# A bound on the row gathers of two attention stages, with padding entries that point past the table

## The chip, the cores and the metric

One core of one Trainium2 chip. The metric is the device time of one execution in microseconds (us); the time of a kernel is the median of its runs.

## What is computed

Two layers over a graph of 6,250 nodes with 256 features and 106,250 edges, sorted by destination. Each layer is a graph attention and a mixture of experts, each added to x after a layer norm. The two attentions are what the change touches; cut to that:

```python
def _L0_gnn_ref(x, edge_index, W, att_src, att_dst, bias):       # 4 heads of 64
    h = (x @ W).reshape(N, HEADS, HEAD_DIM)
    e = leaky_relu(a_src[src] + a_dst[dst], 0.2)
    e = exp(e - segment_max(e, dst)[dst])
    alpha = e / segment_sum(e, dst)[dst]
    return segment_sum(alpha[:, :, None] * h[src], dst).reshape(N, 256) + bias

def _L1_gnn_ref(x, edge_attr, W1, W2, att_l, att_r, bias, src, dst):   # 1 head of 256
    score = leaky_relu(er[dst] + el)          # el: from x[src] and edge_attr
    alpha = softmax of score over the edges of one dst
    return segment_sum((x @ W2.T)[src] * alpha[:, None], dst) + bias

x = x + _L0_gnn_ref(_layernorm(x), ...)
x = x + _L0_ffn_ref(_layernorm(x), ...)       # 6 experts, the 2 best
x = x + _L1_gnn_ref(_layernorm(x), ...)
x = x + _L1_ffn_ref(_layernorm(x), ...)       # 8 experts, all
```

## The kernel before

The kernel runs in stages with a barrier after each: `rows(0)`, `attention(0)`, then routing, sorting and the picked experts, `rows(1)`, `attention(1)` and `dense_experts`. All of it is raw code on five engines, each with its own loop, held together by semaphores.

`rows(l)` writes a table `rows_d[l]` to device memory: one row for each node, 260 float32 in stage 0 (4 heads of 64 features, each with its source score) and 257 in stage 1, and one row more, number N = 6250, of zeros (`pad_row`, line 309). `rows(0)` also makes the edge list `edge_pack`: for each edge its source and its destination, and after the 106,250 edges another 256 entries of padding (`pad_pack`, lines 310 and 311) with source N and destination -1.

`attention(l)` takes the destinations in 50 tiles of 125. The edges of one tile are cut into units of 256 (`UE`), and a table holds where each unit starts and which tile it is for. The table has 464 units; those that no tile needs start at entry 106,250, so all their entries are padding. A slot of the loop is 8 units (`U`), and there are 58 slots (`SU`). The work of a slot is spread over five turns of the loop (`LAG`), in buffers for three slots (`RING`):

- SP loads the slot's entries into `pack` and its destinations into `drow`.
- POOL gathers the rows (line 687): 16 indirect DMAs for a slot, two for each unit, each of 128 rows by the 128 source indices of one column of `pack`, into `G`. Before the two gathers of a unit it waits (line 683) until the matmuls that read the same buffer three slots ago are done (`summed`).
- One turn later TensorE transposes the source scores that came with the rows (lines 734 and 735); in stage 0 it waits there for all rows of the slot, in stage 1 VectorE does so, adding the edge's own term (line 967).
- VectorE and ScalarE make a running maximum and the weight of each edge; an entry whose destination is in no tile has zeros in the incidence matrix (`MB`, line 959), so that it adds nothing.
- Two and three turns later TensorE multiplies incidence and weighted rows (line 720), and VectorE merges the sums into `acc` (line 926).

Two other places gather rows by an indirect DMA without any bound: line 1788 (128 rows of 256 float32, the picked experts' inputs) and line 318 (125 rows of 256 float32, in `rows(1)`).

```python
        for u in range(U):
            if late(i, RING):
                after(pool, p + "summed", i * U - U * RING + (u + 1))
            held(pool, p + "pool_seen")
            for q in range(u * C, (u + 1) * C):
                nc.gpsimd.indirect_dma_start(G[:, r, q, :], None, rows_d[l], ...)
```

Of the kernel before, what the change touches and what calls it, by code (L numbers as in the profile page):

```python
# [26 lines left out]
N = 6250  # L27
# [40 lines left out]
def build(nc, a, out):  # L68
    ctx = ExitStack()
    with ctx:  # L70
        def sb(name, shape, dt=F32, scope=ctx):
            return scope.enter_context(nc.sbuf_tensor(name, shape, dt))
# [4 lines left out]
        def S(name):  # L77

            if name not in sems:
                sems[name] = nc.alloc_semaphore(name=f"{name}_{stage[0]}")  # L80
            return sems[name]
# [8 lines left out]
        def after(eng, name, count):  # L90

            if not isinstance(count, int) or count > 0:
                eng.wait_ge(S(name), count)

        def held(eng, name):

            eng.sem_inc(S(name), 1)
# [49 lines left out]
        def late(i, k):  # L147

            return not isinstance(i, int) or i >= k
# [5 lines left out]
        def rows(l, acc, pos_i, share, sc):  # L155
# [6 lines left out]
            p = f"n{l}_"  # L162
# [9 lines left out]
            if l == 0:  # L172
# [6 lines left out]
                pad_pack = sb("pad_pack", [P, C, 2], I32, sc)  # L179
# [45 lines left out]
            with nc.Block() as block:  # L225
# [62 lines left out]
                @block.gpsimd  # L288
                def _(pool):
                    if l == 0:  # L290
                        nc.gpsimd.memset(ident[:, :], 0.0).then_inc(S("ident_zero"), 1)
                        nc.gpsimd.iota(int_n[:, :], pattern=[[1, P]], base=0, channel_multiplier=0)
                        nc.gpsimd.iota(int_nid[:, :], pattern=[[TN, NT]], base=0, channel_multiplier=1)
                        nc.gpsimd.iota(int_base[:, :], pattern=[[TN, NT]], base=0, channel_multiplier=0)
                        nc.gpsimd.iota(int_tile[:, :], pattern=[[1, NT]], base=0, channel_multiplier=0)
                        nc.gpsimd.iota(int_u[:, :], pattern=[[1, KU]], base=0, channel_multiplier=KU).then_inc(S("iotas"), 1)
                        pool.wait_ge(S("ident_zero"), 1)
                        nc.gpsimd.affine_select(out=ident[:, :], in_=ident[:, :], compare_op=ALU.not_equal, fill=1.0,
                                                base=0, pattern=[[-1, P]], channel_multiplier=1)
                        nc.gpsimd.memset(eps_ln[:, :], LN_EPS)  # L300
                        nc.gpsimd.memset(eps_bn[:, :], BN_EPS)
                        nc.gpsimd.memset(ones[:, :], 1.0)
                        nc.gpsimd.memset(zeros[:, :], 0.0)
                        nc.gpsimd.memset(cnt[:, :], 0.0).then_inc(S("fills"), 1)
                        nc.gpsimd.memset(pad_hl[:, 0, :], -1.0)
                        nc.gpsimd.memset(pad_hl[:, 1, :], 0.0)
                        nc.gpsimd.memset(ones_bf[:, :], 1.0)
                        nc.gpsimd.memset(pad_q[:, :], 0.0)
                        nc.gpsimd.memset(pad_row[:, :], 0.0)
                        nc.gpsimd.memset(pad_pack[:, :, 0:1], N)  # L310
                        nc.gpsimd.memset(pad_pack[:, :, 1:2].bitcast(F32), -1.0).then_inc(S("pads_set"), 1)
                    else:
                        for i in range(NG):
                            if i >= 4:
                                pool.wait_ge(S(p + "added"), i - 3)
                            for u in range(GT):
                                for k in range(2):
                                    nc.gpsimd.indirect_dma_start(yg[:, i % 4, u, k, :], None, y_d,
                                                                 bass.IndirectOffsetOnAxis(ap=pos_i[:, i * GT + u, k:k + 1], axis=0)).then_inc(S(p + f"yg_in{i % 4}"), 16)
# [226 lines left out]
        def attention(l, acc, sc):  # L546
# [5 lines left out]
            p = f"g{l}_"  # L552
# [6 lines left out]
            pack = sb(p + "pack", [P, RING, Q, 2], I32, sc)  # L559
# [55 lines left out]
            def run(eng, slot):  # L615

                for i in range(SU + LAG):
                    slot(i, i % RING, i // RING)

            def has(i, lag):  # L620

                return not isinstance(i, int) or lag <= i < SU + lag

            def filled(t, r, k, n):

                return (t + 1 - (k - r + RING - 1) // RING) * n
# [9 lines left out]
            with nc.Block() as block:  # L636
# [37 lines left out]
                @block.gpsimd  # L674
                def _(pool):
                    def slot(i, r, t):
                        if not has(i, 0):
                            return
                        pool.wait_ge(S(p + f"pack_in{r}"), filled(t, r, 0, 16 * U))
                        if isinstance(i, int) and i == RING - 1:  # L680
                            pool.wait_ge(S(p + "tab"), 6)
# [3 lines that stand above are left out]
                            held(pool, p + "pool_seen")  # L685
                            for q in range(u * C, (u + 1) * C):
                                nc.gpsimd.indirect_dma_start(G[:, r, q, :], None, rows_d[l],  # L687
                                                             bass.IndirectOffsetOnAxis(ap=pack[:, r, q, 0:1], axis=0)).then_inc(S(p + f"rows_in{r}"), 16)
                    run(pool, slot)

                @block.tensor
# [1256 lines left out]
```

## Time and profile before

| | us |
|---|---|
| median of 3 runs | 4523.83 (4523.54 to 4540.11) |
| span of the profiled execution | 4519.6 |
| attention stage 0, first to last gather | 174.8 to 1364.7 |
| attention stage 1, first to last gather | 2160.4 to 3348.9 |
| last matmul of the attention sums, stage 0 and 1 | 1416.2 and 3389.5 |

| engine | busy us | share of the span |
|---|---|---|
| TensorE (PE) | 3345.5 | 74% |
| VectorE (DVE) | 2669.4 | 59% |
| ScalarE (ACT) | 1569.3 | 35% |
| GpSimd (POOL) | 2042.6 | 45% |

The trace is of one execution, and its times count from the start of its span; the span is 4.2 us shorter than the median of the runs. A gather's entry on POOL is the time in which the instruction is worked on there, not the time until its rows have landed. "Idle before" is the time in which the engine had nothing to do before an instruction, with what ended it; "issue" there means that nothing the profile shows was waited for.

### The profile page before, as it was taken

To read this page: it belongs to the slowest core of one execution; us is meant where nothing else is said; L and a number is where in the kernel's file an instruction comes from. 1 tells how busy PE (TensorE), PEld (TensorE's weight loads), DVE (VectorE), ACT (ScalarE), POOL (GpSimd) and SP (SyncE) were. 2 spreads that over 40 slices of the span, in tenths; PEclk is the share of its full clock that TensorE was granted. 3 is DMA by queue.
4 is the path that set the end of the run, shared out by engine and by line. 5 is a ranking of instruction groups with operands and counts; after the bars stand their busy time and mean duration, and the time that the engine had idled before them with its cause. 6 is when DMAs were issued, how large, how long until landed. Compare 5 with 4: busy or idle time off the path is not lost. (4 is left out here: it accounts for less than half of the span.)

```text
span 4519.6 us, 72577 instructions
## 1 busy us (share of the span) xinstructions
PE 3345.5 (74%) x16240; PEld 2523.8 (56%) x16240; DVE 2669.4 (59%) x8449; ACT 1569.3 (35%) x4383; POOL 2042.6 (45%) x2095
## 2 busy tenths in 40 slices
PE   4366666666666789966366666666668999999999
PEld 3244444444444577744244444444447888888888
DVE  7489999999987866546356565656555322222221
ACT  2233333333332123332233333333323433343333
POOL 0377777777770033346677777777740000000000
PEclk9667777777776579977677777777778999999999
DMA  3344444444454135534444444444451000000000
GB/s 98 92 105 106 106 107 106 107 107 106 107 98 86 37 122 171 163 102 116 96 107 107 105 106 106 105 106 106 106 66 60 8 5 7 7 5 7 5 7 7
DMA packets 382598, 369.83 MB, mean 82 GB/s; under 512 B 249324, under 2 KB 309388, under 8 KB 382242
## 3 DMA queue, kind: packets, MB, share of 16 engines
q0 software_dynamic: 107072, 272.84, 24.4%
q1 hardware_dynamic: 272774, 92.39, 8.5%
q8 instruction: 102, 1.67, 0.2%
q14 instruction: 254, 2.08, 0.1%
q10 hardware_dynamic: 2396, 0.84, 0.1%
HBM read 324.13 MB, written 41.59 MB: 81 GB/s over the span
## 5 line engine op out<-in xcount | busy, mean ns | idle before, releaser
L687 POOL DMA_INDIRECT g_G<-rows,g_pack x1856 | 1807.9, 974 | 771.7 <-issue 487.0
L720 PE MATMUL bank<-g_G,g_MB 128*125 128x260 f32 x1856 | 663.3, 504 | 230.4 <-DVE acc L926 229.2
L926 DVE SCALAR_TENSOR_TENSOR acc<-acc,g_c,bank 125x65 f32 (+1 forms) x2320 | 618.5, 316 | 146.3 <-PE bank L720 71.1
L720 PE MATMUL bank<-g_G,g_M 128*125 128x257 f32 x1856 | 633.5, 489 | 20.7 <-DVE acc L926 20.5
L1367 DVE SCALAR_TENSOR_TENSOR X<-bank,e_cw,X 125x256 f32 (+1 forms) x400 | 175.2, 479 | 795.8 <-PE bank L1193 795.8
L720 PEld LDWEIGHTS bank<-g_G,g_MB 128*125 128x125 f32 x1856 | 422.8, 246 | 373.2 <-DVE acc L926 265.9
L1263 ACT ACTIVATE e_h<-bank,e_bi_c,e_sc_c 128x250 f32<-128x250 f32 x800 | 403.6, 555 | 560.6 <-PE bank L1184 422.3
L791 ACT ACTIVATE g_mt_d<-bank,unode 125x256 bf16<-125x256 f32 x928 | 381.9, 461 | 444.7 <-PE bank L705 444.5
L720 PEld LDWEIGHTS bank<-g_G,g_M 128*125 128x125 f32 x1856 | 418.1, 241 | 147.4 <-DVE acc L926 26.2
L1193 PE MATMUL bank<-e_w,e_h 128*125 128x256 f32 x1600 | 379.0, 380 | 3.1 <-ACT e_h L1263 3.1
L1184 PE MATMUL bank<-e_h,e_w 128*128 128x250 f32 x1600 | 377.8, 378 | 1.2 <-ACT e_h L1263 1.2
L1175 PE MATMUL bank<-e_xnT,e_w 128*128 128x250 f32 x1600 | 372.9, 375 | 0.0
L803 ACT ACTIVATE g_MT<-g_mt_d,ones 125x512 bf16<-125x512 bf16 x464 | 335.1, 722 | 11.4
L1193 PEld LDWEIGHTS bank<-e_w,e_h 128*125 128x125 f32 x1600 | 299.8, 187 | 47.5 <-ACT e_h L1263 3.9
L1175 PEld LDWEIGHTS bank<-e_xnT,e_w 128*128 128x128 f32 x1600 | 304.3, 190 | 36.5 <-issue 0.7
L1184 PEld LDWEIGHTS bank<-e_h,e_w 128*128 128x128 f32 x1600 | 297.7, 191 | 42.5 <-issue 8.0
L825 ACT COPY g_LT<-bank 64x128 f32<-64x128 f32 (+1 forms) x116 | 29.7, 256 | 833.2 <-PE bank L735 827.2
L959 DVE TENSOR_TENSOR g_MB<-iota_b,g_dloc 128x500 f32<-128x500 bf16 (+1 forms) x464 | 302.5, 674 | 0.1
L942 DVE TENSOR_TENSOR g_G<-g_G,bank 128x1024 f32<-128x1024 f32 x232 | 280.9, 1211 | 0.5 <-ACT bank L831 0.5
L734 PE MATMUL bank<-ident,g_b 128*16 128x128 f32 x58 | 21.5, 371 | 315.5 <-DVE g_dloc L972 301.0
L1788 POOL DMA_INDIRECT x_xg<-expert_in,ids x108 | 107.0, 990 | 288.6 <-PE bank L1804 190.4
L769 PE MATMUL bank<-g_rhs,g_MT 125*128 125x24 bf16 (+1 forms) x1856 | 66.3, 174 | 226.8 <-DVE g_rhs L1063 119.1
(299 smaller groups left out, 4151.2 us busy)
## 6 DMA issues: line engine op xcount, KB each, us to landing
g_G<-rows,g_pack POOLq DMA_INDIRECT x1856
acc<-in_edge_attr SPq DMA_DIRECT2D x50, 531.2 KB
g_pack<-edge_pack SPq DMA_DIRECT2D x928, 2.0 KB
g_drow<-edge_dst SPq DMA_DIRECT2D x928, 1.0 KB
expert_out<-x_y SPq DMA_DIRECT2D x54, 256.0 KB
g_qe<-edge_q SPq DMA_DIRECT2D x464, 1.0 KB
rows<-acc SPq DMA_DIRECT2D x25, 253.9 KB
rows<-n_T SPq DMA_DIRECT2D x25, 251.0 KB
```

The costliest lines, as they stand in the source:

```text
L687: nc.gpsimd.indirect_dma_start(G[:, r, q, :], None, rows_d[l], bass.IndirectOffsetOnAxis(ap=pack[:, r, q, 0:1], axis=0)).then_inc(S(p + f" ...
L720: mm_ = nc.tensor.matmul(sum_bank(r, k, u)[0:TN, 0:HW], left, G[:, rk, q, :], start=(c == 0), stop=(c == C - 1))
L791: ins = nc.scalar.activation(mt_d[:, v_ % 2, k * C:(k + 1) * C, :], bank[2 + v_ % 2][0:TN, k * UE:(k + 1) * UE].rearrange("p (e c) -> p c ...
L803: nc.scalar.activation(MT[:, turn(r, 1, v_), :, :], mt_d[:, v_ % 2, :, :], ACT.Relu, bias=ones[0:TN, 0:1], scale=-1.0).then_inc(S(p + "MT" ...
L926: ins = nc.vector.scalar_tensor_tensor(at, at, c1[:, rk, u, h:h + 1], sum_bank(r, k, u)[0:TN, h * W:(h + 1) * W], ALU.mult, ALU.add)
L942: ins = nc.vector.tensor_tensor(g[:, :, 0:DH], g[:, :, 0:DH], w, ALU.mult)
L959: nc.vector.tensor_tensor(MB[:, r, at, :], iota_b[:, 0:TN].unsqueeze(1).broadcast_to([P, CP, TN]), dloc[:, r, at, 0:1].broadcast_to([P, CP ...
L1175: mm = nc.tensor.matmul(bank[m][:, 0:GN], w1[:, e, k, m * P:(m + 1) * P], xnT[:, r, k, :], start=(k == 0), stop=(k == 1))
L1184: mm = nc.tensor.matmul(bank[2 + m][:, 0:GN], w2[:, e, k, m * P:(m + 1) * P], h1[:, k, :], start=(k == 0), stop=(k == 1))
L1193: mm = nc.tensor.matmul(bank[4 + u][0:TN, 0:D], h2[:, e % 2, k, u * TN:(u + 1) * TN], w3[:, e, k, :], start=(k == 0), stop=(k == 1))
L1263: ins = nc.scalar.activation((h1 if q == 0 else h2[:, e % 2, :, :])[:, m, :], bank[2 * q + m][:, 0:GN], ACT.Relu, bias=bi_c[:, q, m, e:e + ...
L1367: ins = nc.vector.scalar_tensor_tensor(xt, bank[4 + u][0:TN, 0:D], cw[:, r, u, e:e + 1], xt, ALU.mult, ALU.add)
```

## The change

The padding's source index becomes N + 1, and each gather of both attention stages gets a bound of N with the order to pass over an index beyond it instead of reporting an error. The row of an index that is passed over is not fetched, and its place in `G` keeps what it held. In the built program each of the 1,856 gathers has one instruction more ahead of it on POOL's queue: a register is set to 6250, and the gather names that register as its bound. No other instruction is added, removed or moved on any engine.

```diff
-                        nc.gpsimd.memset(pad_pack[:, :, 0:1], N)
+                        nc.gpsimd.memset(pad_pack[:, :, 0:1], N + 1)
...
                                 nc.gpsimd.indirect_dma_start(G[:, r, q, :], None, rows_d[l],
-                                                             bass.IndirectOffsetOnAxis(ap=pack[:, r, q, 0:1], axis=0)).then_inc(S(p + f"rows_in{r}"), 16)
+                                                             bass.IndirectOffsetOnAxis(ap=pack[:, r, q, 0:1], axis=0),
+                                                             bounds_check=N, oob_is_err=False).then_inc(S(p + f"rows_in{r}"), 16)
```

## Rows read from the trace of the kernel before

**Rows 1.** Windows: 400 us in the middle of stage 0 and stage 1, all engines.

```profile
core 0: us, PE busy (x) PEld busy (x) DVE busy (x) ACT busy (x) POOL busy (x), PEclk, DMA share, GB/s
300.00:700.00 400.00, 274.53 (x1406) 177.92 (x1407) 361.86 (x1262) 154.29 (x489) 304.63 (x314) 0.76 0.43 106
2600.00:3000.00 400.00, 260.75 (x1398) 170.16 (x1397) 241.51 (x826) 142.48 (x463) 304.93 (x313) 0.75 0.45 106
```

**Rows 2.** Timeline of POOL in stage 0: start us, us, engine, line, operation [idle before].

```profile
584.13 0.95 POOL L687 DMA_INDIRECT g_G<-rows,g_pack  x1 [0.30 <-issue]
585.38 0.95 POOL L687 DMA_INDIRECT g_G<-rows,g_pack  x1 [0.30 <-issue]
586.63 0.94 POOL L687 DMA_INDIRECT g_G<-rows,g_pack  x1 [0.30 <-issue]
...
590.38 1.22 POOL L687 DMA_INDIRECT g_G<-rows,g_pack  x1 [0.30 <-issue]
```

**Rows 3.** Groups of instructions of POOL: its three kinds of gathers.

```profile
L687 POOL DMA_INDIRECT g_G<-rows,g_pack x1856 | 1807.9, 974 | 771.7 <-issue 487.0 <-DMA g_pack<-edge_pack 201.3 <-PE bank L720 83.4
L318 POOL DMA_INDIRECT n_yg<-expert_out,pos_i x100 | 124.2, 1242 | 78.8 <-POOLq L88 48.6 <-issue 29.9 <-DVEq L473 0.3
L1788 POOL DMA_INDIRECT x_xg<-expert_in,ids x108 | 107.0, 990 | 288.6 <-PE bank L1804 190.4 <-POOLq L88 80.2 <-issue 18.0
```

**Rows 4.** Windows of line 687, stage 0, ordinary stretch and end.

```profile
core 0: us, POOL busy (x), PEclk, DMA share, GB/s
...
700.00:1100.00 400.00, 304.28 (x315) 0.76 0.43 107
...
1324.00:1345.00 21.00, 15.82 (x18) 0.74 1.00 80
1345.00:1365.00 20.00, 13.31 (x14) 0.67 1.01 82
```

**Rows 5.** Windows of line 687, stage 1, ordinary stretch and end.

```profile
2600.00:3000.00 400.00, 304.93 (x313) 0.75 0.45 106
...
3307.00:3349.00 42.00, 29.66 (x31) 0.71 0.97 79
```

**Rows 6.** Timeline of TensorE, stage 0: line 734 in the last turns, and one turn's last sums.

```profile
1283.76 0.42 PE L734 MATMUL bank<-ident,g_G 128*64 128x128 f32 x1
...
1305.20 0.42 PE L734 MATMUL bank<-ident,g_G 128*64 128x128 f32 x1
...
1325.46 0.42 PE L734 MATMUL bank<-ident,g_G 128*64 128x128 f32 x1
...
1351.80 0.41 PE L734 MATMUL bank<-ident,g_G 128*64 128x128 f32 x1 [5.88 <-DMA g_G<-rows,g_pack]
...
1368.89 2.09 PE L720 MATMUL bank<-g_G,g_MB 128*125 128x260 f32 x4 [1.24 <-DVE acc L926]
1378.19 0.41 PE L734 MATMUL bank<-ident,g_G 128*64 128x128 f32 x1 [7.21 <-DMA g_G<-rows,g_pack]
```

**Rows 7.** Timeline of POOL at the end of stage 0.

```profile
1354.97 0.95 POOL L687 DMA_INDIRECT g_G<-rows,g_pack  x1 [2.70 <-PE bank L720]
...
1363.72 0.94 POOL L687 DMA_INDIRECT g_G<-rows,g_pack  x1 [0.30 <-issue]
```

**Rows 8.** Timeline of VectorE, stage 1: line 967 in the last turns.

```profile
3286.43 0.18 DVE L967 TENSOR_TENSOR g_b<-g_G,g_qe 128x16 f32<-128x16 f32 x1 [2.73 <-DMA g_G<-rows,g_pack]
3307.83 0.18 DVE L967 TENSOR_TENSOR g_b<-g_G,g_qe 128x16 f32<-128x16 f32 x1 [3.31 <-DMA g_G<-rows,g_pack]
3335.72 0.18 DVE L967 TENSOR_TENSOR g_b<-g_G,g_qe 128x16 f32<-128x16 f32 x1 [10.14 <-DMA g_G<-rows,g_pack]
3361.42 0.18 DVE L967 TENSOR_TENSOR g_b<-g_G,g_qe 128x16 f32<-128x16 f32 x1 [7.09 <-DMA g_G<-rows,g_pack]
```

**Rows 9.** Timeline of POOL in stage 1: around slot 56's first gather, and at the end.

```profile
3304.08 1.25 POOL L687 DMA_INDIRECT g_G<-rows,g_pack  x1 [0.30 <-issue]
3305.64 0.95 POOL L687 DMA_INDIRECT g_G<-rows,g_pack  x1 [0.31 <-issue]
...
3339.16 0.94 POOL L687 DMA_INDIRECT g_G<-rows,g_pack  x1 [3.35 <-PE bank L720]
...
3347.90 0.95 POOL L687 DMA_INDIRECT g_G<-rows,g_pack  x1 [0.30 <-issue]
```

**Rows 10.** Three lines with their gathers: duration ns min/median/max, first and last start us.

```profile
L687 POOL DMA_INDIRECT g_G<-rows,g_pack x1856: 942/946/1780, 174.8 to 3347.9; - x186
...
L318 POOL DMA_INDIRECT n_yg<-expert_out,pos_i x100: 1180/1202/1716, 1976.5 to 2129.7; - x100
...
L1788 POOL DMA_INDIRECT x_xg<-expert_in,ids x108: 940/946/1747, 1612.6 to 1927.0; - x108
```

## Prediction, made before the changed kernel ran

> **What bounds the kernel now.** I read the engine table first, then the gathers' line, then windows of the two attention stages, then the ends of these stages in order of time. The engine table's averages mix stages, so these are read apart. [rows 1] is one stretch in the middle of each attention stage. In 400 us POOL starts 314 gathers in stage 0 and 313 in stage 1, the same number, although VectorE has much more to do in stage 0 (361.86 us against 241.51). The same pace under so different a load points at POOL. [rows 2] shows why: gathers stand back to back, 0.95 us each and 0.30 us between them, every sixteenth one 1.22 us. The 314 gathers of stage 0 are busy for 304.63 us, and 314 x 0.30 = 94.2 us of gaps make 398.8 of the 400 us. So POOL issues gathers without a rest, 400 / 314 = 1.274 us apiece, 16 to a slot of the loop: 20.4 us a slot. Everything else in both stages has room to spare: in stage 0 VectorE is nearest, at 361.86 of 400 us (90%).
>
> The whole list of gathers is one line [rows 3]: 1,856 of them, 974 ns in the mean. This is the number to keep: **whatever is added to one gather is multiplied by 1,856**, and nothing hides it.
>
> The padding is at the end only. Counted from the inputs (50 tiles of 125 destinations, each rounded up to whole units of 256 entries), the list fills 448 units and the table has 464; 16 empty units are exactly the last two slots, 56 and 57, of each stage, and unit 447 holds 139 padding entries. So the padding is 16 x 256 + 139 = 4,235 entries a stage, in 33 of 928 gathers, and all of them fetch the same row N. [rows 4] and [rows 5] show what this does: the DMA engines' share goes from 0.43 and 0.45 to 1.00, while the bytes moved fall from 106 to 80 GB/s. Reading one row over and over costs the DMA engines about three times as much a byte as reading scattered rows (1.00 / 80 against 0.43 / 106), and near the end they no longer keep up with POOL. That is what the change can win.
>
> **What it can win, stage by stage.** In stage 0, TensorE starts a turn with the transposes at line 734 [rows 6]. The starts of 1283.76, 1305.20 and 1325.46 us are 21.4 and 20.3 us apart; then come 1351.80 and 1378.19, 26.3 and 26.4 us apart, and there TensorE waits 5.88 and 7.21 us for gathered rows. At the ordinary pace of 20.4 us the last start would be 1325.46 + 2 x 20.4 = 1366.3, which is 11.9 us earlier. The two waits themselves, 13.1 us, are the upper end. POOL would allow it: it stood 2.70 us before one gather of slot 57 [rows 7], of which 2.40 us came from the late sums, and its last gather ended at 1364.66. Without that it ends at 1362.3, and with 2.5 us to land (below) the rows are there at 1364.8. I take 11.9, the ordinary pace.
>
> In stage 1 VectorE's sum at line 967 waits for the rows of each slot [rows 8]: 2.73 us before 3286.43, which is the ordinary wait for POOL's pace, then 3.31, 10.14 and 7.09 us. The starts at 3307.83, 3335.72 and 3361.42 are 27.9 and 25.7 us apart. At 20.4 us the last would be 3348.6, 12.8 us earlier. Check from POOL's side: slot 57's last gather ended at 3348.85 after a wait of 3.35 us [rows 9], so it could have ended at 3345.8. The landing time is seen at slot 55: its sixteen gathers end, counted back 33 from the last, at about 3305.3, and line 967 starts at 3307.83, 2.5 us later. So slot 57 could start at 3348.3. I take 12.8.
>
> What follows the last start in each stage (three more turns of merging, then the barrier) is the same work and shifts as it stands. The gain is 11.9 + 12.8 = **24.7 us**, 0.55%, if a gather with the bound costs POOL what one without it costs.
>
> **What is added.** Three things.
> 1. One register move ahead of each gather, 1,856 in all, on POOL's queue. The trace has a neighbour for it: between every second pair of gathers a semaphore instruction stands already (the wait for the sums), and the gap is 0.30 us with it and without it [rows 2]. So an instruction of the queue is hidden behind the 0.95 us in which the previous gather is worked on. Cost 0; the gaps are given to 0.01 us, so the upper bound is 1,856 x 0.01 = 19 us. The cover goes only if the gather must wait for its register; no row shows that.
> 2. The comparison of 128 indices with the bound. No gather before has one. Lower end: the three kinds of gathers without a check. The 128-row ones of lines 687 and 1788 have the same median, 946 ns, though their rows have 1,040 or 1,028 and 1,024 bytes [rows 3, 10]: the 0.95 us is per index, not per byte, and a comparison that the list's loop makes at any rate adds nothing. Upper end: the gather at line 318 has 125 indices, fewer, and takes 1,202 ns, 256 ns more [rows 10]. So POOL does have a dearer way through a list that is not the regular one, and a list with holes might take it: 1,856 x 0.256 = 475 us. A gain here is excluded for the 1,823 gathers that have no padding: they build the same 128 descriptors.
> 3. The 33 padding gathers of each stage may get shorter on POOL, since they build fewer descriptors, or none. At most that takes POOL away as the bound of slots 56 and 57. Stage 0 wins little by it: TensorE's work and waits in the turn from 1351.80, without the wait for rows, last until 1370.98 [rows 6], 19.2 us against 20.4. Lower end 0, upper end some 3 us in stage 0 and 8 us in stage 1, where VectorE's turn is 12 us. I take 0, because the row nearest to it, the 125-row gather, has fewer indices and is not shorter.
>
> For 2 I take the lower end, 0, as the nearest row in shape: 128 indices of the same list, same stride, same tile. I do so with less than even confidence, and the upper end stays in the range.
>
> A rule of the Trainium skill speaks against the change at this point. GPSIMD Engine Reference, section 3.1, says that branching on data costs some 12 cycles an element on these cores; at the 1.2 GHz it states, 128 elements would be 1.28 us a gather by this estimate, and the sum +2,376 us. No gather before branches on an index, so the trace does not show it; the 946 ns of a whole gather [rows 10] only say that the present loop has no such step.
>
> **Sum.** The profiled execution has a span of 4519.6 us, and the median of the runs is 4523.83, 4.2 us above it: launch and end lie around the span. 4519.6 - 24.7 = 4494.9; with the 4.2 us, **4499.1 us**. About 0.5% (22.6 us) is what a measurement of this kernel can tell from no change, so the forecast is just past that line.
>
> **The rivals.**
> - *The comparison costs POOL time* (slower). Place: the 1.25 us from gather to gather, which is the pace of both stages. Price: 1,856 times c, less 24.7 us. It decides from c = 24.7 / 1,856 = 13 ns: beyond that the kernel is slower, beyond 25 ns by over 0.5%. At 50 ns (5% of a gather) the time is 4499.1 + 92.8 = 4592; at 110 ns 4703; at the 256 ns of the 125-row gather 4974. For it: the margin is tiny against 946 ns, and a dearer way exists. Against it: the check is one comparison beside an address computed for each index. Chance 0.38.
> - *Branch for each index.* The loop over the list takes a step of its own for each index, as if the list were gone through twice: another 946 ns a gather [rows 10], 1,856 x 0.946 = 1755.8 us, 6254.9 us in all. For it: nothing in the trace; against it: not even the dearer list of line 318 is near. Chance 0.03. By the Trainium skill's page GPSIMD Engine Reference, section 3.1, it would be some 6875 us, an estimate.
> - *The entries are not left out on the DMA side*, or the end of the stage is held by something else. Then nothing is won: 4519 to 4526 us. For it: a wait is put down to the transfer that came last, and another may stand right behind it; and an entry beyond the bound may still be fetched from somewhere. Against it: the excess wait names the gathered rows in both stages. Chance 0.11.
> - *The padding gathers get short on POOL* as well (point 3): up to 11 us more, 4488. Chance 0.06.
>
> **How the numbers follow.** The forecast has 0.42: own range 4494 to 4504 (the gain 20 to 30 us by the bounds above). About two thirds of it lie past 0.5%: 0.28; with the short padding gathers 0.06, faster is 0.34. Within 0.5%: the rest of the forecast 0.14, no gain 0.11, a comparison of 13 to 25 ns 0.02, together 0.27. Slower: 0.36 and 0.03, 0.39. Cases of both signs hold most of the chance, so the range is wide: from 4488, the short padding gathers, up to 4703, a comparison of 110 ns; above that lie the dearest rows and the branch, 0.17 together, and some 0.02 lie below.
>
> **What would show it.** First the median of the gathers at line 687 and the gap between them: 946 ns and 0.30 us say that check and move are free; each nanosecond more is 1.9 us. Then the DMA share in the last 40 us of each stage: it should not go to 1.00. Then the waits for rows at lines 734 and 967 in the last two turns: gone, or at the ordinary 2 to 3 us. Last, POOL's gathers of slots 56 and 57: 0.95 us or less. I am wrong if gathers without padding have grown, or if the last turns are still 26 us apart with the DMA engines idle.

## The result, and the profile after

The changed kernel takes 4602.82 us (median of 4 runs, 4599.39 to 4607.97) against 4528.55 us for the kernel before in the runs beside it (4 runs, 4523.54 to 4540.11). The ratio is 1.0142, with a 95% interval of 1.0125 to 1.0159: **slower by 1.4%**, where 0.55% faster was forecast. The profiled execution has a span of 4603.2 us, 83.6 us above that of the kernel before.

The line of the gathers, which answers to [rows 3] and [rows 10], first as a group (busy us, mean ns, idle before) and then with its minimum, median and maximum in ns:

```profile
L687 POOL DMA_INDIRECT g_G<-rows,g_pack x1856 | 1920.3, 1035 | 764.8 <-issue 675.0 <-PE bank L721 62.8 <-DMA g_pack<-edge_pack 27.1
```

```profile
L687 POOLq MOVE  x1856: 29/29/38, 175.0 to 3432.1; - x186
L687 POOL DMA_INDIRECT g_G<-rows,g_pack x1856: 995/1002/1789, 175.9 to 3443.1; - x186
```

The median of a gather went from 946 to 1,002 ns, 56 ns more. The register moves are there, 29 ns each, on POOL's queue. The gaps are as in [rows 2]; the timeline of POOL in the same stretch:

```profile
583.61 1.00 POOL L687 DMA_INDIRECT g_G<-rows,g_pack  x1 [0.30 <-issue]
584.91 1.00 POOL L687 DMA_INDIRECT g_G<-rows,g_pack  x1 [0.30 <-issue]
586.22 1.00 POOL L687 DMA_INDIRECT g_G<-rows,g_pack  x1 [0.31 <-issue]
```

So it is the gather itself that grew, and not what stands between two gathers. The windows of [rows 1] show a slower pace, 295 and 304 gathers in 400 us instead of 314 and 313. The median's 56 ns alone would give some 300 in either stage; how the two stages differ stands at the end of the part on the prediction:

```profile
core 0: us, PE busy (x) PEld busy (x) DVE busy (x) ACT busy (x) POOL busy (x), PEclk, DMA share, GB/s
300.00:700.00 400.00, 281.53 (x1322) 176.60 (x1322) 344.97 (x1204) 142.71 (x455) 310.40 (x295) 0.67 0.40 100
...
2600.00:3000.00 400.00, 256.69 (x1368) 167.99 (x1366) 234.28 (x795) 139.51 (x456) 307.71 (x304) 0.74 0.44 102
```

The ends of the stages did what the change was to do. The waits for rows at TensorE's transposes (line 735 now, stage 0) and at VectorE's sum (line 968, stage 1), which answer to [rows 6] and [rows 8]:

```profile
1392.97 0.41 PE L735 MATMUL bank<-ident,g_G 128*64 128x128 f32 x1 [1.37 <-DMA g_G<-rows,g_pack]
...
1413.77 0.41 PE L735 MATMUL bank<-ident,g_G 128*64 128x128 f32 x1 [0.89 <-DMA g_G<-rows,g_pack]
...
1435.04 0.41 PE L735 MATMUL bank<-ident,g_G 128*64 128x128 f32 x1 [1.67 <-DMA g_G<-rows,g_pack]
```

```profile
3403.49 0.18 DVE L968 TENSOR_TENSOR g_b<-g_G,g_qe 128x16 f32<-128x16 f32 x1 [2.72 <-DMA g_G<-rows,g_pack]
3424.35 0.18 DVE L968 TENSOR_TENSOR g_b<-g_G,g_qe 128x16 f32<-128x16 f32 x1 [2.74 <-DMA g_G<-rows,g_pack]
3445.22 0.18 DVE L968 TENSOR_TENSOR g_b<-g_G,g_qe 128x16 f32<-128x16 f32 x1 [2.73 <-DMA g_G<-rows,g_pack]
```

The last turns are 20.8 to 21.3 us apart instead of 26 to 28, and the waits are 0.9 to 2.7 us instead of 6 to 10. The windows of the gathers at the end of stage 1, which answer to [rows 5], show that the padding is no longer fetched, and that POOL works on those gathers as on any other:

```profile
3380.00:3400.00 20.00, 15.43 (x16) 0.76 0.44 104
3400.00:3420.00 20.00, 15.43 (x16) 0.76 0.11 12
3420.00:3440.00 20.00, 15.43 (x16) 0.76 0.03 2
```

In the last window 16 gathers take 15.43 us of POOL, as 20 us earlier, while the DMA engines are busy for 3% and move 2 GB/s.

### The profile page after: what moved, and what is told of

It is laid out like the page before. It is cut to its first block and busy times, and to the rows that moved or that the text cites. A ratio compares the mean times of both kernels' runs of the same rounds, so it can differ in the third digit from the quotient of the medians.

```text
span 4603.2 us, 74433 instructions
## 1 busy us (share of the span) xinstructions
PE 3408.6 (74%) x16240; PEld 2540.6 (55%) x16240; DVE 2675.1 (58%) x8449; ACT 1570.3 (34%) x4383; POOL 2156.6 (47%) x2095
## 5 line engine op out<-in xcount | busy, mean ns | idle before, releaser
L687 POOL DMA_INDIRECT g_G<-rows,g_pack x1856 | 1920.3, 1035 | 764.8 <-issue 675.0
L721 PE MATMUL bank<-g_G,g_MB 128*125 128x260 f32 x1856 | 712.0, 535 | 152.8 <-DVE acc L927 151.2
L721 PEld LDWEIGHTS bank<-g_G,g_MB 128*125 128x125 f32 x1856 | 452.1, 262 | 315.7 <-DVE acc L927 178.0
L826 ACT COPY g_LT<-bank 64x128 f32<-64x128 f32 (+1 forms) x116 | 29.8, 257 | 930.8 <-PE bank L736 930.8
```

The lines of the kernel that those rows point to most:

```text
L721: mm_ = nc.tensor.matmul(sum_bank(r, k, u)[0:TN, 0:HW], left, G[:, rk, q, :], start=(c == 0), stop=(c == C - 1))
```

## The experiments

The theory after this: testing the bound costs POOL 56 ns in each gather, whatever the indices are, and leaving the padding out wins some 25 us at the two ends. Two rivals: the register move costs, or the price belongs to leaving out rows. The first four kernels below were timed in one comparison; the kernel before had a median of 4531.74 us there (14 runs, 4513.99 to 4543.16), while the expectations count from the 4523.83 us of its earlier runs.

**The bound without padding beyond it.** Edit to the changed kernel:

```diff
-                        nc.gpsimd.memset(pad_pack[:, :, 0:1], N + 1)
+                        nc.gpsimd.memset(pad_pack[:, :, 0:1], N)
```

> The changed kernel with the padding's index back at N: the bound is tested in every gather, no index is beyond it, so nothing is left out and all padding entries fetch row N again. Theory (the test itself costs POOL about 56 ns a gather whatever the indices are, and leaving the rows out wins about 25 us at the two stage ends): gathers at 1,002 ns in the median as in the changed kernel, the last two turns of each stage 26 us apart again, total about 25 us above the changed kernel, 4,628 us. Rival (the price belongs to leaving out rows, as a mode of the list with holes): gathers at 946 ns and about 4,524 us, as before.

Measured: 4632.8 us (4 runs, 4632.0 to 4636.93), ratio to the kernel before 1.0222 (1.0199 to 1.0245). The gathers' line and the last turns of stage 0:

```profile
L687 POOL DMA_INDIRECT g_G<-rows,g_pack x1856: 995/1002/1787, 174.7 to 3460.6; - x186
```

```profile
1386.60 0.41 PE L735 MATMUL bank<-ident,g_G 128*64 128x128 f32 x1 [2.74 <-DMA g_G<-rows,g_pack]
1414.16 0.41 PE L735 MATMUL bank<-ident,g_G 128*64 128x128 f32 x1 [7.25 <-DMA g_G<-rows,g_pack]
1440.73 0.41 PE L735 MATMUL bank<-ident,g_G 128*64 128x128 f32 x1 [6.53 <-DMA g_G<-rows,g_pack]
```

The price is there in full although no row is left out, 1,002 ns, and the long waits at the end are back (27.6 and 26.6 us from start to start). The price belongs to the bound on the gather and not to leaving rows out. What leaving out wins is the distance to the changed kernel, 4632.8 - 4602.8 = 30 us. The changed kernel was timed in another comparison; against the kernel with one register (below), which was timed in this one and is as fast as the changed one, it is 26.6 us.

**Padding over different rows, no bound.** Edit to the kernel before:

```diff
-                        nc.gpsimd.memset(pad_pack[:, :, 0:1], N)
+                        nc.gpsimd.iota(pad_pack[:, :, 0], pattern=[[1, C]], base=0, channel_multiplier=C)
```

> The kernel before, without any bound, with the padding's 256 indices set to rows 0 to 255 instead of all to row N. Theory (the two stage ends are held up because 4,235 fetches of one and the same row are slow): gathers stay at 946 ns, the DMA share no longer goes to 1.00 at the ends, the waits for rows there fall to the ordinary 2 to 3 us, and the time is 24.7 us under the kernel before, about 4,499 us. Rival (the ends are slow because so many rows are fetched at all, or for another reason): no change, 4,524 us.

Measured: 4511.25 us (6 runs, 4506.87 to 4513.49), ratio 0.9951 (0.9934 to 0.9968), that is 15 to 30 us less. The forecast gain of 24.7 us lies in that interval; the forecast time, 4,499 us, was 12 us too low. The gathers, the last turns of stage 0, and windows of the gathers at its end:

```profile
L687 POOL DMA_INDIRECT g_G<-rows,g_pack x1856: 942/949/1787, 176.3 to 3347.1; - x186
```

```profile
1337.59 0.41 PE L734 MATMUL bank<-ident,g_G 128*64 128x128 f32 x1 [1.48 <-DMA g_G<-rows,g_pack]
1358.20 0.40 PE L734 MATMUL bank<-ident,g_G 128*64 128x128 f32 x1 [1.44 <-DMA g_G<-rows,g_pack]
1378.73 0.40 PE L734 MATMUL bank<-ident,g_G 128*64 128x128 f32 x1 [1.66 <-DMA g_G<-rows,g_pack]
```

```profile
1324.00:1345.00 21.00, 16.04 (x17) 0.67 0.42 107
1345.00:1365.00 20.00, 15.21 (x16) 0.66 0.37 101
```

The padding is fetched as before, as many rows and bytes, at 101 to 107 GB/s and a DMA share of 0.4 where [rows 4] have 80 to 82 GB/s and 1.00. So the ends were slow because one row was fetched over and over, and not because of the number of fetches. In this one trace the gain of stage 0 does not show as a sum, since the gathers of stage 0 took 13 us more of POOL than in the trace of before (917.89 against 904.96 us in all), mostly the longer ones among them; the timed runs carry the verdict. **This version beats both kernels**, the kernel before by about 0.5%, and it needs no bound.

**The bound on the last slots alone.** Edit to the changed kernel (it relies on the padding of these inputs, which begins in slot 55):

```diff
-                                                             bounds_check=N, oob_is_err=False)
+                                                             **(dict(bounds_check=N, oob_is_err=False) if i >= SU - 3 else {}))
```

> The changed kernel with the bound on the gathers of slots 55 to 57 alone, where all the padding of these inputs lies: 96 gathers with the test instead of 1,856. Theory: the test's price falls to 96 x 0.056 = 5 us and the gain at the ends stays, so about 4,504 us; gathers of the first 55 slots at 946 ns. Rival (the price hangs on the program having the bounded form at all, not on each gather): 4,603 us as the changed kernel.

Measured: 4513.74 us (9 runs, 4508.91 to 4521.23), ratio 0.9959 (0.9944 to 0.9973), 18 us under the kernel before beside it. The gathers' line, and POOL's timeline where slot 55 begins:

```profile
L687 POOL DMA_INDIRECT g_G<-rows,g_pack x1856: 942/949/1786, 176.4 to 3352.1; - x186
L687 POOLq MOVE  x96: 29/29/38, 1304.1 to 3340.3; - x96
```

```profile
1312.40 0.95 POOL L687 DMA_INDIRECT g_G<-rows,g_pack  x1 [0.30 <-issue]
1313.66 0.95 POOL L687 DMA_INDIRECT g_G<-rows,g_pack  x1 [0.30 <-issue]
1314.91 1.01 POOL L687 DMA_INDIRECT g_G<-rows,g_pack  x1 [0.30 <-issue]
1316.22 1.01 POOL L687 DMA_INDIRECT g_G<-rows,g_pack  x1 [0.30 <-issue]
...
1320.70 1.00 POOL L687 DMA_INDIRECT g_G<-rows,g_pack  x1 [0.30 <-issue]
```

With 96 tests instead of 1,856 the loss is gone and the gain stays. The step from 0.95 to 1.00 us comes with the first gather that has the bound, at 1314.91, before any padding. The price hangs on each gather that has the bound.

**One register.** Edit to the changed kernel:

```diff
                 def _(pool):
+                    limit = pool.to_reg(N)
...
-                                                             bounds_check=N, oob_is_err=False)
+                                                             bounds_check=limit, oob_is_err=False)
```

> The changed kernel with the bound in one register that is set once, instead of a register move ahead of each of the 1,856 gathers; the test stays. Theory (the test costs, the 29 ns move is hidden behind the gather before): gathers at 1,002 ns, gaps at 0.30 us, 4,603 us as the changed kernel. Rival (the move, or the wait for a register just written, is what costs): gathers back at 946 ns or gaps below 0.30 us, and up to 100 us less, 4,499 us.

Measured: 4606.16 us (4 runs, 4597.21 to 4610.15), ratio 1.016 (1.0135 to 1.0184), as the changed kernel.

```profile
L689 POOL DMA_INDIRECT g_G<-rows,g_pack x1856: 995/1002/1786, 174.5 to 3441.0; - x186
```

Without the 1,856 moves nothing changes, not even a gather's length: the moves cost nothing, as forecast. The bound still comes from a register here, so this run does not tell reading the register from testing against it.

**An index beyond the bound as an error.** One run, no interval. The kernel with the bound and no padding beyond it, with one word changed:

```diff
-                                                             bounds_check=N, oob_is_err=False)
+                                                             bounds_check=N, oob_is_err=True)
```

> The kernel with the check alone (padding index N, bound N) and the other way to treat an index beyond the bound: report an error instead of passing over it. Theory (the comparison costs): gathers at 1,002 ns and about 4,630 us, as with the check alone. Rival (the price is that of being ready to pass over rows): gathers at 946 ns, about 4,530 us.

```profile
L687 POOL DMA_INDIRECT g_G<-rows,g_pack x1856: 1007/1015/1787, 175.8 to 3465.3; - x186
```

1,015 ns, 13 ns more than with passing over; 4636.98 us in one run. So it is not the readiness to pass over that costs, and a gather that would report an error is a little dearer still. In the traces all gathers together took 1936.86 us against 1916.17 us with passing over; one run's time is too little to show these 21 us.

**What the price goes by.** One run. One gather more at the start of 16 slots of stage 1, into a spare tile:

```diff
+            if l == 1:
+                probe = sb("probe", [P, HW], F32, sc)
...
+                        k = i - 20
+                        if l == 1 and 0 <= k < 16:
+                            n = (32, 64, 96, 125)[k // 2 % 4]
+                            nc.gpsimd.indirect_dma_start(probe[0:n, :], None, rows_d[1], bass.IndirectOffsetOnAxis(ap=pack[0:n, r, 0, 0:1], axis=0),
+                                                         **(dict(bounds_check=N, oob_is_err=False) if k % 2 else {})).then_inc(S("probed"), 16)
+                            pool.wait_ge(S("probed"), 16 * k + 16)
```

> The kernel before with one gather more at the start of each of 16 slots of stage 1, into a spare tile, which POOL waits for: of 32, 64, 96 and 125 indices, in turn without and with the bound (no index beyond it). The 16 gathers and the waits for them lengthen the run by some 16 x 4 = 64 us; only their durations count. If the price is one comparison for each index: 56 ns at 128, so 14 ns at 32, 28 at 64, 42 at 96 and 55 at 125. If it is a fixed price of a gather with a bound: 56 ns at every length. The unbounded one of 125 tells whether the 1,202 ns of line 318 come from its number of indices (then 1.2 us here) or from its own place (then some 0.93).

The timeline of POOL, these gathers alone; 32, 64, 96 and 125 indices, each first without the bound and then with it:

```profile
2581.16 0.87 POOL L687 DMA_INDIRECT probe<-rows,g_pack  x1 [0.30 <-issue]
...
2604.51 0.92 POOL L687 DMA_INDIRECT probe<-rows,g_pack  x1 [0.31 <-issue]
...
2628.51 0.91 POOL L687 DMA_INDIRECT probe<-rows,g_pack  x1 [0.30 <-issue]
...
2651.89 0.96 POOL L687 DMA_INDIRECT probe<-rows,g_pack  x1 [0.30 <-issue]
...
2675.53 0.92 POOL L687 DMA_INDIRECT probe<-rows,g_pack  x1 [0.30 <-issue]
...
2699.10 0.97 POOL L687 DMA_INDIRECT probe<-rows,g_pack  x1 [0.30 <-issue]
...
2722.74 1.21 POOL L687 DMA_INDIRECT probe<-rows,g_pack  x1 [0.30 <-issue]
...
2748.01 1.26 POOL L687 DMA_INDIRECT probe<-rows,g_pack  x1 [0.30 <-issue]
```

The bound costs 0.05 us at every length, so it is a fixed price of a gather and not one comparison for each index. The second row of eight gathers has the same steps within 0.01 us. (The run took 4592.92 us, 69 us more than the one run of the kernel before beside it, 4523.9 us; some 64 were expected for the 16 waits.)

**The same price elsewhere.** One run. A bound that no index exceeds on the gathers of lines 1788 and 318, and none on the attention's:

```diff
-                                                         bass.IndirectOffsetOnAxis(ap=ids[:, 2 * k + u:2 * k + u + 1], axis=0))
+                                                         bass.IndirectOffsetOnAxis(ap=ids[:, 2 * k + u:2 * k + u + 1], axis=0),
+                                                         bounds_check=N - 1, oob_is_err=False)
...
-                                                                 bass.IndirectOffsetOnAxis(ap=pos_i[:, i * GT + u, k:k + 1], axis=0))
+                                                                 bass.IndirectOffsetOnAxis(ap=pos_i[:, i * GT + u, k:k + 1], axis=0),
+                                                                 bounds_check=XTILES * XT - 1, oob_is_err=False)
```

> The kernel before with a bound that no index exceeds on the two other kinds of gathers, 108 of 128 rows at line 1788 and 100 of 125 rows at line 318, and none on the attention's. If each bounded gather pays the same: medians of 1,002 and about 1,257 ns, and some 5 us more in all, since POOL issues the 100 back to back and the 108 stand in a stage in which it waits for TensorE (190 us). If the price depends on what else runs: other steps than 56 ns.

```profile
L1789 POOL DMA_INDIRECT x_xg<-expert_in,ids x108: 992/998/1604, 1607.6 to 1919.9; - x108
```

```profile
L318 POOL DMA_INDIRECT n_yg<-expert_out,pos_i x100: 1242/1261/1747, 1968.2 to 2128.3; - x100
```

52 and 59 ns more than in [rows 10] (946 and 1,202 ns), in stages with other work beside them. What these cost the kernel can't be told from this run: its 4515.44 us lie among the runs of the kernel before (4513.99 to 4543.16).

## Why the prediction was wrong

- *POOL's gathers set the pace of both stages, and what is added to one is multiplied by 1,856*: right. No gap between two gathers of a stage is over 0.32 us in the changed kernel, in stage 0 too, where VectorE had been busy for 90% of the time. The median's step of 56 ns does not give each stage by itself, though (below).
- *The register move is hidden, cost 0*: the cost is right. It takes 29 ns, and taking the moves away changed nothing. The cover was not the one gather before it: with the bound on the last slots alone, the first move is at 1304.1 us and the first gather with a bound starts at 1314.91, some 11 us or eight gathers later.
- *The comparison, taken at 0*: **this is the step that failed.** The ends were 0 and 256 ns, and the lower one was taken because the 128-row gathers are nearest in shape. But those rows are gathers without the bound; that they agree with each other says nothing of a gather with it. The measured value is 56 ns in the median, 1,856 x 0.056 = 103.9 us. That rival had a chance of 0.38, and the stated range holds the measured time because of it; the way that was forecast, faster, was wrong. The rival's own formula with 56 ns gives 4499.1 + 103.9 = 4603.0 us, and 4602.82 were measured. That it fits so closely is luck: in the traces the gathers grew by 1920.3 - 1807.9 = 112.4 us and the gain was 29.8 us, not 24.7, and the kernel before took 4528.55 us beside the changed one, not 4523.83.
- *The mechanism named for it* (one comparison beside each address) was wrong too: the price is fixed for a gather, 0.05 us at 32 indices as at 125. So was the reading that the 0.95 us of a gather is "per index": 32 indices take 0.87 us. What POOL does in the 0.05 us is not shown.
- *The upper end from the 125-row gather*: the 256 ns go with the count of 125 and not with the place. The gather of 125 indices takes 1.21 us in the attention stage too, without any bound, and with one it pays the same 0.05 us more. Why 125 indices take longer than 128 is not shown.
- *The branch for each index*: excluded. By the Trainium skill, GPSIMD Engine Reference, section 3.1, branching on data costs some 12 cycles an element; the bounded gather of 128 costs 56 ns more, so that rule does not describe this test.
- *The gain at the ends, 24.7 us*: the right mechanism, a little small. From POOL's last gather to the last merge of the stage it was 1418.26 - 1364.66 = 53.6 us before and 1474.63 - 1433.78 = 40.9 us after in stage 0, and 41.2 and 29.6 us in stage 1: 24.3 us. With it go POOL's own waits for the late sums, 2.4 and 3.05 us. Together 29.8 us; the runs with the bound on every gather gave 26.6 to 30 us. The rival by which the entries would be fetched all the same is excluded by the DMA share of 0.03 in the last window.
- *The count of gathers with padding* was off, and nothing hangs on it: the 139 padding entries of unit 447 lie in both of its gathers, so 34 gathers of a stage have padding, not 33, and 1,788 of the 1,856 have none, not 1,823.
- *Padding gathers do not get shorter on POOL*: right. They take 1.00 us with nothing to fetch. The Trainium skill's page DMA: Bandwidth & Descriptors, Anatomy of one DMA, says that many descriptors can be emitted before it shows; the trace agrees from 32 indices (0.87 us) to 128 (0.946 us), though not at 125.

The traces add up. From the first gather to the end of the last one, stage 0 took 1257.9 us instead of 1189.9 and stage 1 1227.3 instead of 1188.4: 106.9 us more. After the last gathers, to stage 1's first gather and to the end of the span, it is 24.4 us less, and the first gather of all starts 1.1 us later. Together that is the 83.6 us.

The two stages did not grow alike. The sums of the gathers at line 687 in stage 0 and stage 1, before and then after:

```profile
core 0: us, POOL busy (x), PEclk, DMA share, GB/s
170.00:1500.00 1330.00, 904.96 (x928) 0.73 0.43 103
2150.00:3480.00 1330.00, 902.91 (x928) 0.74 0.45 100
```

```profile
core 0: us, POOL busy (x), PEclk, DMA share, GB/s
170.00:1500.00 1330.00, 975.42 (x928) 0.67 0.38 97
2150.00:3480.00 1330.00, 944.88 (x928) 0.73 0.41 96
```

928 x 56 ns would be 52.0 us a stage. Stage 0 grew by 70.5 us and stage 1 by 42.0 us, which is 76 and 45 ns a gather in the mean. In stage 1 the other kernels agree: 902.95 us without the bound (the padding over different rows), 945.56 and 945.88 us with it (no padding beyond it, and one register). In stage 0 two kernels without the bound already differ by 13 us (904.96 and 917.89), mostly by gathers longer than the rest. What makes these long is not shown, so the 56 ns hold for the median gather, and the price of a whole stage is known to some 15 us only.

## What to carry to other kernels

When one engine issues the same instruction without a rest, an option on that instruction is priced at its count, not at the few cases it is for: here 68 gathers with padding in two stages could win 27 to 30 us, and 1,856 tests cost over 100. Where no row shows the instruction with the option, the agreement of rows without it is no estimate of zero; take a value inside the bounds. And padding that must be read should point at different rows: that won 0.5% here for one changed line.

## What the runs showed of the hardware

- Reading one row of device memory over and over kept the DMA engines busy for 1.00 of the time at 80 GB/s; as many fetches spread over 256 rows took 0.4 at 101 to 107 GB/s.
- The length of a gather on POOL hardly goes by its number of indices: 0.87 us at 32, 0.91 at 64, 0.92 at 96, 0.946 at 128, but 1.21 at 125. A bound on the indices adds 0.05 us at each of these.
- In stage 0 TensorE's granted clock was 0.76 of full speed in the middle stretch (300 to 700 us) of the kernel before, and 0.66 to 0.67, a mean between its levels of 1.2 and 2.4 GHz, in the four kernels with the bound on all of the attention's gathers. Before, TensorE began a turn with a wait for rows 2 times between 700 and 1100 us (1.5 us in all), and in the changed kernel 18 times (32.8 us); the mean matmul of the sums went from 504 to 535 ns. It cost no time in the changed kernel's stage 0 that the trace shows, since no gap between its gathers is over 0.32 us. Why the clock fell was not tried.
